# Decoder layer, self attention: the causal mask moved from TensorE products to VectorE's row maximum, on negated scores

## The chip, the cores and the metric

The kernel runs on one core of one Trainium2 chip. The metric is the device time of one execution in microseconds (us), the median of three runs; lower is better.

## What is computed

The reference is one decoder layer over x of shape (4, 1024, 256), float32. Its three parts are a causal self attention, a cross attention over 77 context rows, and a block with latent attention and four experts. Only the first part is changed:

```python
x = x + _L0_attn_ref(_layernorm(x), gamma, w_qkv, w_out)
...
def _L0_attn_ref(x, gamma, w_qkv, w_out):      # 8 heads of 128, 1024 rows
    ...
    q = q * scale_attn                          # 128 ** -0.5
    sim = jnp.einsum('bihd,bjhd->bhij', q, k)
    causal_mask = jnp.triu(jnp.ones((n, n), dtype=bool), k=1)
    sim = jnp.where(causal_mask, neg, sim)
    attn = jax.nn.softmax(sim, axis=-1)
    out = jnp.einsum('bhij,bjhd->bihd', attn, v)
```

## The kernel before

The four batches are worked through one after the other; each passes through self attention, cross attention, latent attention and routing, and after the last batch the expert layers run over all sorted rows. Every engine has an instruction stream of its own, in an order written out by hand, and counts semaphores to wait for the others.

**Self attention.** A batch has 8 heads, numbered 0 to 7. One head has 8 query tiles t = 0 to 7 of 128 rows. Only the causal part of the scores is computed: tile t has n = 128(t+1) columns. For each head TensorE (PE) projects q and k (L910) and v (L920) from the transposed rows. For each tile, `scores` (L926) waits until the exponentials of tile t-2 are done (L933), multiplies q by k into one or two PSUM banks (L937), and adds the causal mask to the last 128 columns by one more product in bf16, of an identity and a 128x128 upper triangle of -3e38 (L940). There are two buffers of two banks each, so tiles t and t+2 share one. A float32 product is two matrix instructions in the trace, and a transpose and the bf16 mask product are one each.

VectorE (DVE) takes the maximum of the n columns, negated, straight from PSUM (`tile_max`, L1424, L1428). ScalarE (ACT) then computes exp(score - maximum) from PSUM into SBUF with its row sum (L744, in `self_exps`). VectorE takes the reciprocal of the sum (L1434) and scales the tile (L1439). In VectorE's order (`head`, L1449) the maximum of tile t stands ahead of the reciprocal and scaling of tile t-1.

**What lies between.** From head 1 on, PE does a piece of the previous head's `products` (L968) after each tile's scores: it transposes 128x128 blocks of the probabilities (`turn_probs`, L955), ScalarE copies them to SBUF (`take_probs`, L735), and PE multiplies them with v (`use_probs`, L965). A head has 12 such pieces u, one in tile 0, one or two in every other. ScalarE's order has the pieces of tile t ahead of the exponential of tile t. After tile 7, PE projects the next head (L910, L920) and ScalarE copies the results out (L719, L723).

**The two ends of a batch.** Head 0 has nothing between its eight tiles (L983). After head 7's tiles PE waits until VectorE has taken head 6's output (L1012, released by L1445, which stands behind head 7's last scaling), then does head 7's products alone.

**Latent attention** masks in VectorE already: `max_chunk` (L1604) uses `tensor_reduce` for full banks (L1618) and, for the last columns, `tensor_tensor_reduce` with `causal_wide` (L1623), a 128x512 float32 constant, which is zero but for the triangle in its last 128 columns. It writes the sum to a scratch tile in SBUF and the maximum to a column.

**The start.** SyncE's queue loads x, then the four tensors of `first_consts` (L222, L483), two heads' weights, and all the other constants, `causal_wide` the first of them. VectorE waits for the other constants at L1400, ahead of head 0.

## Time and profile before

| | |
|---|---|
| median of 3 runs | 2685.35 us (2682.97 to 2687.71) |
| the profiled execution's own time | 2685.82 us |
| its span, first to last instruction | 2684.1 us |
| mean granted TensorE clock | 0.971 |
| PE matmul busy | 2520.5 us (94%) |
| DVE busy | 1383.6 us (52%) |
| ACT busy | 1065.1 us (40%) |
| POOL busy | 313.0 us (12%) |
| chain that ended last, by engine | PE 89%, ACT 3%, issue 3%, DVE 3% |
| mask products, L940 | 256 (4 batches x 8 heads x 8 tiles) |

The profile is of one execution. Matrix instructions overlap each other, so an instruction's duration is longer than the time until the next one starts: what a product costs the engine is read from start to start. "Issue" is time in which an engine waited for nothing that the profile shows. The granted clock is 1 at 2.4 GHz and 0.5 at 1.2 GHz.

### The profile page before, as it was taken

The page shows a single profiled execution, that of the slowest core. Times are in us where ns is not written, and L with a number is a line of the kernel's source. Part 1 is how long each engine was busy: PE and PEld are TensorE (multiplying, and loading weights), DVE is VectorE, ACT ScalarE, POOL GpSimd, SP SyncE. Part 2 cuts the span into 40 slices and gives each one's busy share as a digit, 9 for nine tenths or more (in the row PEclk, how much of TensorE's full clock was granted, in tenths as well). Part 3 has the DMA queues.
Part 4 walks back from the last instruction along what each step waited for, and adds up shares of the span by engine and source line. Part 5 has one row for each costly group of instructions (what it writes and reads, how often), then busy time and mean ns, then how long its engine had stood idle before and what let it go on. Part 6 is the DMA issues. An engine that isn't in the chain of part 4 may idle for free.

```text
span 2684.1 us, 44027 instructions
## 1 busy us (share of the span) xinstructions
PE 2520.5 (94%) x16830; PEld 1680.7 (63%) x16831; DVE 1383.6 (52%) x3834; ACT 1065.1 (40%) x2284; POOL 313.0 (12%) x436
## 2 busy tenths in 40 slices
PE   7999899998999999998999999989999999969998
PEld 4555665664555675664655675655556665649997
DVE  3334377853333477843333477833333578744443
ACT  3444134643444134543444134534443225612221
POOL 2000010212000010211000010220000011231111
PEclk9999999998999999998999999999999999979999
DMA  3000000001000000001000000010000000041111
GB/s 106 13 12 1 16 1 1 2 15 44 12 13 1 16 1 2 2 18 39 15 10 1 16 1 2 2 41 23 12 7 1 16 1 2 2 188 57 53 53 38
DMA packets 33490, 57.30 MB, mean 21 GB/s; under 512 B 7915, under 2 KB 24504, under 8 KB 32920
## 3 DMA queue, kind: packets, MB, share of 16 engines
q1 hardware_dynamic: 28552, 41.73, 5.0%
q0 software_dynamic: 4752, 13.02, 1.3%
q8 instruction: 126, 2.06, 0.3%
q14 instruction: 60, 0.49, 0.1%
HBM read 40.41 MB, written 14.32 MB: 20 GB/s over the span
## 4 chain that ended last, share of the span: by engine, by line
PE 89%; ACT 3%; issue 3%; DVE 3%; another core or an unknown queue 1%; POOL 1%; DMA 0%; DVEq 0%; POOLq 0%
PE ps L1221 11%; PE ps L965 10%; PE ps L937 9%; PE ps L910 8%; PE ps L1251 6%; PE ps L895 6%; PE ps L955 5%; PE ps L1326 5%; PE ps L1340 5%; PE ps L920 4%; PE ps L1186 4%; PE ps L850 3%; PE ps L866 2%; PE ps L1086 1%; PE ps L1070 1%
## 5 line engine op out<-in xcount | busy, mean ns | idle before, releaser
L1428 DVE TENSOR_REDUCE neg_max<-ps 128x1 f32<-128x128 f32 (+7 forms) x256 | 194.1, 758 | 597.6 <-PE ps L940 555.4
L803 ACT ACTIVATE arena<-ps 128x512 f32<-128x512 f32 (+1 forms) x640 | 320.1, 552 | 276.1 <-PE ps L1221 273.3
L1221 PE MATMUL ps<-arena 32*128 32x256 f32 (+1 forms) x2560 | 386.9, 379 | 0.0
L1221 PEld LDWEIGHTS ps<-arena 32*128 32x128 f32 x2560 | 272.9, 184 | 111.8 <-issue 72.3
L1186 PE MATMUL ps<-arena 32*128 32x512 f32 (+3 forms) x1536 | 334.7, 527 | 3.9 <-ACT arena L793 3.9
L937 PE MATMUL ps<-arena 128*128 128x512 f32 (+3 forms) x768 | 304.8, 509 | 25.6 <-ACT arena L744 18.5
L965 PE MATMUL ps<-arena 128*128 128x512 f32 (+3 forms) x768 | 319.2, 503 | 5.5 <-ACT arena L735 1.7
L735 ACT ACTIVATE arena<-ps 128x512 f32<-128x512 f32 (+3 forms) x384 | 188.0, 491 | 296.2 <-PE ps L955 294.2
L937 PEld LDWEIGHTS ps<-arena 128*128 128x128 f32 x768 | 143.9, 197 | 164.3 <-issue 130.6
L910 PE MATMUL ps<-turned_t,arena 128*128 128x512 f32 x512 | 227.7, 598 | 1.1 <-ACT turned_t L706 1.1
L744 ACT ACTIVATE arena<-ps,neg_max 128x128 f32<-128x128 f32 (+7 forms) x256 | 189.0, 738 | 65.6 <-DVE neg_max L1428 46.1
L955 PE MATMUL ps<-ident,arena 128*128 128x128 f32 x1152 | 191.6, 276 | 20.8 <-ACT arena L723 11.4
L955 PEld LDWEIGHTS ps<-ident,arena 128*128 128x128 f32 x1152 | 131.4, 141 | 114.6 <-issue 83.5
L1251 PE MATMUL ps<-arena,mv_rows 128*32 128x256 f32 (+1 forms) x2560 | 188.4, 369 | 2.7 <-POOL arena L646 2.7
L1618 DVE TENSOR_REDUCE arena<-ps 128x1 f32<-128x512 f32 x256 | 164.7, 685 | 42.7 <-PE ps L1186 40.9
L910 PEld LDWEIGHTS ps<-turned_t,arena 128*128 128x128 f32 x512 | 95.7, 192 | 111.2 <-issue 109.7
L646 POOL TENSOR_SCALAR_AFFINE_SELECT arena<-arena 128x1024 f32<-128x1024 f32 x64 | 71.2, 1113 | 606.7 <-ACT arena L803 606.7
L1623 DVE CUSTOM_DVE_ANT_0 arena<-ps,causal_wide 128x128 f32<-128x128 f32 (+3 forms) x256 | 113.1, 488 | 53.6 <-PE ps L1186 53.1
L719 ACT ACTIVATE arena<-ps 128x512 f32<-128x512 f32 x128 | 76.4, 597 | 157.6 <-PE ps L910 154.2
L1623 DVE CUSTOM_DVE_ANT_0 arena<-ps,causal_wide,arena 128x128 f32<-128x128 f32 (+3 forms) x256 | 127.4, 548 | 22.2 <-PE ps L1186 21.6
L580 POOL TENSOR_TENSOR tmp<-mv,c_eps 128x4 f32<-128x4 f32 x34 | 6.8, 201 | 1131.6 <-DVE mv L1376 1131.5
L965 PEld LDWEIGHTS ps<-arena 128*128 128x128 f32 x768 | 116.7, 192 | 34.5 <-issue 17.7
(218 smaller groups left out, 3667.3 us busy)
## 6 DMA issues: line engine op xcount, KB each, us to landing
arena<-in_w_qkv SPq DMA_DIRECT2D x32, 384.0 KB, 3.0
arena<-in_w SPq DMA_DIRECT2D x2, 4096.0 KB, 16.6
xin<-in_x SPq DMA_DIRECT2D x5, 1024.0 KB, 5.6
xres_ids<-sorted_res SPq DMA_DIRECT2D x35, 129.0 KB, 2.3
xin<-sorted_rows SPq DMA_DIRECT2D x35, 128.0 KB
w_out<-in_w_out SPq DMA_DIRECT2D x1, 1024.0 KB
out<-xin,out_row POOLq DMA_INDIRECT x35, 2.9
sorted_res<-xin SPq DMA_DIRECT2D x4, 129.0 KB
```

What stands on the lines that cost most here:

```text
L735: nc.scalar.activation(probs_t[u % 4][:, lo:BANK], ps[:, 4 + u % 2, lo:BANK], ACT.Copy).then_inc(pt_taken, 1)
L744: nc.scalar.activation(probs[par][:, TRI[t]:TRI[t] + n], ps[:, buf:buf + 2, :].rearrange("p a n -> p (a n)")[:, 0:n], ACT.Exp, bias=neg_ma ...
L803: nc.scalar.activation(mprobs_t[n % BUFS][:, j, 0:QUARTER + more], ps[:, item_bank(n, j), 0:QUARTER + more], ACT.Exp).then_inc(mexp_done, 1)
L910: last = nc.tensor.matmul(ps[:, 4 + i % 3, :], w_head[par][:, kt, w:w + HD], turned_t[:, kt, (i % 2) * BANK:(i % 2 + 1) * BANK], start=(kt ...
L937: last = nc.tensor.matmul(ps[:, buf + c // BANK, 0:m], q_t[par][:, t * P:(t + 1) * P], k_t[par][:, c:c + m], start=True, stop=True)
L955: last = nc.tensor.transpose(ps[:, 4 + u % 2, (t - 4 * g) * P:(t - 4 * g + 1) * P], probs[par][:, TRI[t] + kb * P:TRI[t] + (kb + 1) * P], ...
L965: nc.tensor.matmul(ps[:, 6 + g, lo:BANK], v_rows[par][:, kb, :], probs_t[u % 4][:, lo:BANK], start=(kb == 0), stop=True, skip_group_check= ...
L1186: last = nc.tensor.matmul(ps[:, MAX_BANK[m], at:at + n], q_heads_t[rows_j, g, t * P:(t + 1) * P], k_heads_t[rows_j, g, c * BANK:c * BANK + ...
L1221: return nc.tensor.matmul(ps[:, item_bank(n, j), kb * QUARTER:kb * QUARTER + n_q], k_heads_t[rows_j, g, keys_at:keys_at + P], q_heads_t[ro ...
L1251: last = nc.tensor.matmul(ps[SLOT * j:SLOT * (j + 1), 7, QUARTER - n_q:QUARTER], mv_rows[:, 2 * p + kb, GROUP * g + j, :], mprobs_t[n % BU ...
L1428: nc.vector.tensor_reduce(neg_max[:, par, t:t + 1], ps[:, buf:buf + 2, :].rearrange("p a n -> p (a n)")[:, 0:n], AX.X, ALU.max, negate=Tru ...
L1623: last = nc.vector.tensor_tensor_reduce(max_junk[s % 2][:, at:at + n], scores, causal_wide[:, BANK - n:BANK], 1.0, part if c == 1 else MAS ...
```

## The change

The 256 mask products go. ScalarE scales q by -(128 ** -0.5) when it copies it, so PSUM holds negated scores. VectorE adds `causal_wide`, whose triangle now is +3e38, in place in PSUM and takes the row minimum in the same instruction, which is the negated maximum. For tiles 4 to 7, whose columns fill two banks, it first takes the minimum of the full first bank (`tensor_reduce` into `low_part`), waits for that on its own semaphore, and gives it to the second instruction as its starting value. ScalarE's exponential takes scale -1. Latent attention's masked maximum subtracts the constant instead of adding it. Two bf16 constants and their loads ahead of the first weights go.

```diff
@@ constants
-        ident_b = sb("ident_b", [P, P], BF16)
-        causal_b = sb("causal_b", [P, P], BF16)
...
-        first_consts = [(ident, "ident"), (gamma, "gamma"), (ident_b, "ident_b"), (causal_b, "causal_b")]
+        first_consts = [(ident, "ident"), (gamma, "gamma")]
...
+        low_part = sb("low_part", [P, 2])
...
+        low_done = sem("low_done")
@@ take_qkv, ScalarE
                         nc.scalar.activation(dst, ps[:, 4 + i % 3, :], ACT.Copy,
-                                             scale=float(HD) ** -0.5 if i < 2 else 1.0).then_inc(qk_taken, 1)
+                                             scale=-float(HD) ** -0.5 if i < 2 else 1.0).then_inc(qk_taken, 1)
@@ self_exps, ScalarE
-                                             bias=neg_max[:, par, t:t + 1],
+                                             bias=neg_max[:, par, t:t + 1], scale=-1.0,
                                              accum_out=row_sum[:, par, t:t + 1]).then_inc(exp_done, 1)
@@ scores, TensorE
                         m = min(BANK, n - c)
-                        diag = c + m == n
                         last = nc.tensor.matmul(ps[:, buf + c // BANK, 0:m], q_t[par][:, t * P:(t + 1) * P],
                                                 k_t[par][:, c:c + m], start=True, stop=True)
-                        if diag:
-                            last = nc.tensor.matmul(ps[:, buf + c // BANK, m - P:m], ident_b[:], causal_b[:],
-                                                    start=False, stop=True, skip_group_check=True)
                     last.then_inc(scores_done, 1)
@@ tile_max, VectorE
                     dve.wait_ge(scores_done, b * (HEADS * NT) + h * NT + t + 1)
-                    nc.vector.tensor_reduce(neg_max[:, par, t:t + 1],
-                                            ps[:, buf:buf + 2, :].rearrange("p a n -> p (a n)")[:, 0:n],
-                                            AX.X, ALU.max, negate=True).then_inc(max_done, 1)
+                    if t >= HALF:
+                        nc.vector.tensor_reduce(low_part[:, t % 2:t % 2 + 1], ps[:, buf, :], AX.X, ALU.min).then_inc(low_done, 1)
+                        dve.wait_ge(low_done, b * (HEADS * HALF) + h * HALF + t - HALF + 1)
+                        n -= BANK
+                        buf += 1
+                    nc.vector.tensor_tensor_reduce(ps[:, buf, 0:n], ps[:, buf, 0:n], causal_wide[:, BANK - n:BANK], 1.0,
+                                                   low_part[:, t % 2:t % 2 + 1] if t >= HALF else -MASKED, ALU.add, ALU.min,
+                                                   neg_max[:, par, t:t + 1]).then_inc(max_done, 1)
@@ max_chunk, VectorE (latent attention)
-                                                                  part if c == 1 else MASKED, ALU.add, ALU.max,
+                                                                  part if c == 1 else MASKED, ALU.subtract, ALU.max,
@@ arrange, on the host
-        "ident_b": bf16_bits(np.eye(P)),
-        "causal_b": bf16_bits(upper),
-        "causal_wide": np.concatenate([np.zeros((P, BANK - P), np.float32), upper], 1),
+        "causal_wide": np.concatenate([np.zeros((P, BANK - P), np.float32), -upper], 1),
```

## Rows read from the trace of the kernel before

**Rows 1.** The chain of waits from 56 to 267 us (batch 0, heads 1 to 7)
```profile
by line: PE ps L965 27.6%; PE ps L937 25.0%; PE ps L910 19.5%; PE ps L955 13.9%; PE ps L920 10.2%; ACT arena L723 2.0%; PE ps L940 1.3%; issue 0.6%
```
**Rows 2.** The timeline of one head, 150.9 to 173.5 us: start, duration, instruction, idle before
```profile
151.79 0.66 PE L955 MATMUL ps<-ident,arena 128*128 128x128 f32 x4 [0.41 <-ACT arena L723]
152.49 0.60 ACT L735 ACTIVATE arena<-ps 128x512 f32<-128x512 f32 x1 [0.74 <-PE ps L955]
...
153.23 1.10 PE L965 MATMUL ps<-arena 128*128 128x512 f32 x2
...
167.40 0.22 PE L940 MATMUL ps<-causal_b,ident_b 128*128 128x128 bf16 x1
167.46 0.50 PE L955 MATMUL ps<-ident,arena 128*128 128x128 f32 x3
167.66 1.09 DVE L1428 TENSOR_REDUCE neg_max<-ps 128x1 f32<-128x896 f32 x1 [1.94 <-PE ps L940]
...
168.66 0.15 DVE L1434 RECIPROCAL inv_sum<-row_sum 128x1 f32<-128x1 f32 x1
168.78 1.01 ACT L744 ACTIVATE arena<-ps,neg_max 128x896 f32<-128x896 f32 x1 [0.30 <-DVE neg_max L1428]
168.85 0.62 DVE L1439 TENSOR_SCALAR arena<-arena,inv_sum 128x768 f32<-128x768 f32 x1
...
170.85 0.38 ACT L735 ACTIVATE arena<-ps 128x256 f32<-128x256 f32 x1 [0.96 <-PE ps L955]
```
**Rows 3.** Groups of VectorE instructions, shapes kept apart: count, busy us, mean ns, idle before
```profile
L1618 DVE TENSOR_REDUCE arena<-ps 128x1 f32<-128x512 f32 x256 | 164.7, 685 | 42.7 <-PE ps L1186 40.9
L1623 DVE CUSTOM_DVE_ANT_0 arena<-ps,causal_wide,arena 128x512 f32<-128x512 f32 x64 | 45.5, 749 | 14.1 <-PE ps L1186 14.1
...
L1623 DVE CUSTOM_DVE_ANT_0 arena<-ps,causal_wide 128x512 f32<-128x512 f32 x64 | 42.0, 689 | 17.6 <-PE ps L1186 17.3
...
L1428 DVE TENSOR_REDUCE neg_max<-ps 128x1 f32<-128x1024 f32 x32 | 39.2, 1225 | 33.2 <-PE ps L940 33.1
...
L1428 DVE TENSOR_REDUCE neg_max<-ps 128x1 f32<-128x640 f32 x32 | 26.4, 825 | 64.4 <-PE ps L940 63.4 <-remote 1.0
...
L1623 DVE CUSTOM_DVE_ANT_0 arena<-ps,causal_wide,arena 128x128 f32<-128x128 f32 x64 | 22.3, 348 | 2.8 <-PE ps L1186 2.8
L1428 DVE TENSOR_REDUCE neg_max<-ps 128x1 f32<-128x512 f32 x32 | 22.1, 692 | 20.1 <-PE ps L940 15.8 <-remote 4.4
```
**Rows 4.** The timeline of batch 0's head 0, 40 to 44 us
```profile
40.78 0.48 DVE L1439 TENSOR_SCALAR arena<-arena,inv_sum 128x512 f32<-128x512 f32 x1
...
41.27 0.96 DVE L1428 TENSOR_REDUCE neg_max<-ps 128x1 f32<-128x768 f32 x1
...
42.26 0.90 ACT L744 ACTIVATE arena<-ps,neg_max 128x768 f32<-128x768 f32 x1 [0.67 <-DVE neg_max L1428]
...
43.31 1.98 PE L937 MATMUL ps<-arena 128*128 128x512 f32 x4
```
**Rows 5.** The timeline behind the last tile of batch 0's head 7
```profile
269.25 0.68 DVE L1445 COPY arena<-ps 128x512 f32<-128x512 f32 x1
270.04 0.96 PE L955 MATMUL ps<-ident,arena 128*128 128x128 f32 x7 [2.35 <-issue]
```
**Rows 6.** Busy time and granted clock (PEclk) of a stretch, 272 to 276 us
```profile
272.00:276.00 4.00, 4.00 (x16) 2.71 (x15) 0.34 (x2) 0.38 (x1) 0.00 (x0) 0.57 0.00 0
```
**Rows 7.** The longest pieces of the whole chain: the same projection in batches 1 to 3
```profile
881.69 27.89 PE ps L895 x128
1476.10 27.89 PE ps L895 x128
2066.89 27.89 PE ps L895 x128
```
**Rows 8.** The load of x, from the page's DMA issues: count, KB, us to landing
```profile
xin<-in_x SPq DMA_DIRECT2D x5, 1024.0 KB, 5.6
```

## The prediction

> **What bounds the kernel.** I read the table of busy times and the chain's shares first: PE carries the chain for 89% of the span. Then the chain of waits over the stretch of batch 0 that has heads 1 to 7: the lines on it are PE's, save for one ScalarE copy (L723, 2.0%), and VectorE's maximum is not on it. The mask products are, with 1.3% of 211 us, or 2.7 us for 56 of them, about 0.05 us each [rows 1]. So PE paces this stage and the masks are part of the pace. Then I read the timeline of one head, to find what each mask's removal moves and how much room the longer maximum has; last, the two ends of a batch, where the order of work is different.
>
> **The price of a mask product.** Its row says 0.22 us, but the next transposes start 0.06 us behind it (167.40 to 167.46) [rows 2], and the chain's share gives 0.05. I take 0.055 us. The 256 together are 14.1 us, the most that their removal can give. The weight load of the mask lies beside the product ahead of it and is worth nothing. The Trainium skill ("TensorE: Matmul & The Clock Gate", Back-to-back issue gap) puts a load and a 128-column product at about 81 ns in a sustained stream; here the mask's start to start is 0.06 us and the trace decides. By the page's figure the gain summed below would be some 4 us larger.
>
> **Heads 1 to 6, tiles 2 to 7: gained.** PE's instructions stand shoulder to shoulder around these masks: what follows needs only copies that ScalarE made well before. Six masks a head, 0.33 us.
>
> **Tiles 0 and 1: nothing.** Behind tile 0's mask PE sits idle for 0.41 us until ScalarE has copied v (L723), and that copy hangs on the projection ahead of the scores. A shorter score phase makes this wait longer. Tile 1's mask lies between the transposes of piece 0, whose copy runs from 152.49 to 153.09, and its product at 153.23, which starts 0.14 us after the copy's end; the transposes between, three at 0.11 from 152.78, end at 153.11 [rows 2]. So that product too is timed by ScalarE.
>
> **The new maximum.** Tiles 0 to 3: one masked reduction in place of one reduction. At 512 columns the rows have 0.689 against 0.692 us [rows 3], so no cost. The accumulator's read-out follows each, with its start under the end of the main instruction; I count 0.01 us for it. Tiles 4 to 7: a reduction over 512 columns (0.685), a wait on VectorE's own semaphore, and the form with a starting value from memory. The price of the wait I take from the pair of L1434 and L1439, where the second needs the first: 168.66 + 0.15 = 168.81, second at 168.85, so 0.04 us. Tile 7: 0.685 + 0.04 + 0.749 + 0.01 = 1.484 against 1.225 us, +0.26. Tile 4: 0.685 + 0.04 + 0.348 + 0.01 = 1.083 against 0.825, also +0.26 [rows 2, 3]. The maximum also starts 0.055 us earlier, as no mask product comes between, so ScalarE gets it 0.20 us later against PE's work in tiles 4 to 7.
>
> The Trainium skill ("VectorE: DVE Perf Modes", The DRAIN you can't avoid) says that a semaphore between chained operations costs nothing extra. The trace disagrees: the reciprocal without a wait starts at 168.66 while the maximum (167.66 + 1.09) ends at 168.75, an overlap of 0.09, and the pair with a wait has a gap of 0.04 [rows 2]. By the rule a tile would cost 0.13 us less.
>
> What no row shows is a VectorE write into PSUM. Lower bound: nothing less than the SBUF scratch form (a gain of up to 0.06 a tile, the difference between the forms 0.749 and 0.689, is not excluded). Upper bound: the main instruction takes a second pass, doubling it. The nearest rows are the same instruction with the same PSUM source [rows 3]; I take no surcharge and keep both ends.
>
> **Is it covered in heads 1 to 7?** The exponential of tile 6 waits 0.30 us for the maximum already, ends at about 169.9 with its read-out, and ScalarE is next wanted at 170.85 for a copy that PE needs [rows 2]. Room: about 0.9 us, used: 0.20. The cover is ScalarE's idle time there; were it gone, PE would wait for the copy one for one. In tile 7 the next copy is behind four instructions of the next projection, with a room of about 1 us; in tiles 4 and 5 more, since the exponential of tile 5 stands behind two copies anyway. VectorE is idle 1.94 us ahead of tile 6's maximum. Price: nothing.
>
> **Head 0: a loss.** Here nothing stands between the tiles, and PE waits for exponentials. Three masks lie on the chain ahead of tile 4's maximum (tiles 0, 2, 4), so it starts 0.16 earlier. It lasts 0.26 longer and ends 0.10 later. On VectorE tile 3's scaling follows, and tile 5's maximum stands right behind that: 40.78 + 0.48 = 41.26, start 41.27 [rows 4]. So it starts 0.10 late and ends 0.36 late. Tile 5's exponential, which waits for it (0.67 us), is 0.36 late, and tile 7's scores, which need it and until now started just as PE came free, go from 43.31 to 43.67. Less tile 7's mask, PE leaves head 0 0.30 us later. Times 4 batches: +1.2 us.
>
> **Head 7: a wash.** Five masks (tiles 2 to 6) bring its last scores forward by 0.28 us. Then PE waits for VectorE's L1445 (269.25 + 0.68, PE at 270.04, idle 2.35 us) [rows 5], which follows tile 7's maximum, exponential and scaling. That chain loses 0.055 and gains 0.26. Sum -0.07, times 4: -0.3 us. PE's idle time there grows from 2.35 to about 2.6 us.
>
> **The rest.** Negative scale on ScalarE, subtract for add in latent attention: same instructions, nothing (an effect of either sign would need 0.01 us on each of 512 masked maxima, and these mostly hide under PE). Two loads of 32 KB fewer behind x: x takes 5.6 us for 1024 KB and is issued first [rows 8]; if the loads shared its bandwidth, 64/1024 of 5.6, or 0.35 us. I take nothing. Loads behind them are issued earlier and were not waited for.
>
> **Sum.** Heads 1 to 6: 24 x 0.33 = -7.9. Head 0: +1.2. Head 7: -0.3. Together -7.0 us. Against the profiled execution's 2685.82 us (its span and 1.7 around it) that is 2678.8; that execution was 0.5 above the median, so against the median 2678.3. I say **2678.5**.
>
> **The clock.** After head 7's idle time the clock fell to its lower level, 0.57 on average over 4 us, so 3.4 us at 1.2 GHz, which costs PE 1.7 us [rows 6]. The stretches are not the same in all batches: from projection to projection batch 1 to 2 took 594.4 us and batch 2 to 3 590.8 [rows 7]. Any shift of the work can add or take such a stretch. I count 2 us either way.
>
> **Rivals.**
> 1. *Gain not regained.* PE is paced around the masks by ScalarE's copies, as in tiles 0 and 1, and removal only lengthens waits. For it: it is so in two tiles of eight. Against it: the masks' share of the chain [rows 1]. With half of the 7.9 lost: -3.1, 2682.2. Chance 0.2.
> 2. *The in-place write costs a second pass (slower).* Place: the chain maximum, exponential, scores of head 0, and the end of head 7. At 1.04 ns a column ((0.749 - 0.348)/384) a pass costs 0.29 us in tile 0, 0.56 in tile 2, 0.69 in tile 3, 0.48 in tile 5, 0.61 in tile 6, 0.75 in tile 7. Heads 1 to 6 would still hide it, just (0.20 + 0.61 of the 0.9 us in tile 6). In head 0 tiles 0 and 2 are on the chain, tile 3 stands behind tile 2 on VectorE, and tile 5's scores hang on tile 3: 0.29 + 0.56 + 0.69 + 0.48 = 2.0 us; head 7 adds tile 7's 0.7. Sum: -7.0 + 8.0 + 2.8 = +3.8, 2689.2. It decides from 0.65 of a second pass on (7.0 of 10.8); past a whole one tile 6 shows in 24 heads too. For it: no row shows the write. Against: nothing in the masked form, which also writes 512 columns, costs more than the plain reduction [rows 3]. Chance 0.07.
> 3. *A milder surcharge*, 0.1 to 0.2 us an instruction: by the same four tiles head 0 adds 0.4 to 0.8, head 7 0.1 to 0.2: +2 to +4, so 2680.3 to 2682.3. Chance 0.13.
> 4. *More is gained*: tile 1's mask counts too, and the accumulator pair runs better than its rows. 24 x 0.055 = 1.3 more, and with the 0.13 us of the wait given back in head 0 and 7 about 1 more: -9.3, 2676. Chance 0.1.
> That the masks stay on PE is not possible: their line is gone.
>
> **The numbers.** My forecast, 2676 to 2681, has 0.5. The range 2673.5 to 2685.5 takes in it, rivals 1, 3 and 4 and the clock. About 0.2% (5.4 us) is what a measurement of this kernel can tell from no change; so faster means below 2680.0. Of the forecast 0.42, of rival 4 all 0.1, of rivals 1 and 3 0.04: faster 0.56. Slower (over 2690.7): the part of rival 2 past a whole pass and little else, 0.04. Same: 0.40.
>
> **What would show it.** No L940 in the list; a steady head (scores of tile 0 to the same in the next) shorter by 0.33 us; tile 0's idle time before L955 up from 0.41 to 0.47; masked minimum of 512 columns near 0.69 and 0.75 us; tile 4 to 7's exponentials 0.2 later against PE's work; head 0's projections starting 0.3 later; idle time before L955 at the batch's end 2.6 us. Wrong, if a head is not 0.33 us shorter, or if the in-place form of 512 columns takes over 0.85 us.

## The result, and the profile after

Six executions of each kernel on one chip: 2669.95 us after (2669.04 to 2675.04) against 2684.92 before (2681.45 to 2687.71), ratio 0.9948 with a 95% interval of 0.9935 to 0.9961. That is 15.0 us less (10.5 to 17.5), where 7 were forecast. It is faster by more than the 0.2% bound, and below the range. The profiled execution took 2669.12 us.

The page of the kernel after, its span, the busy times and the shares of the chain:

```profile
span 2667.4 us, 43897 instructions
...
PE 2501.4 (94%) x16574; PEld 1671.2 (63%) x16575; DVE 1417.6 (53%) x4218; ACT 1067.1 (40%) x2284; POOL 312.3 (12%) x436
...
PE 89%; ACT 3%; DVE 3%; issue 3%; POOL 1%; DMA 0%; another core or an unknown queue 0%; SPq 0%; DVEq 0%; POOLq 0%
```

TensorE keeps its 89% of the chain. Lines have moved: scores L936, transposes L951, the products with v L961, the two halves of the maximum L1425 and L1429, VectorE's scaling L1440 and its copy L1446.

The maximum's groups after, shapes kept apart (count, busy us, mean ns, idle before), with latent attention's L1624 for comparison; they answer to [rows 3]:

```profile
L1425 DVE TENSOR_REDUCE low_part<-ps 128x1 f32<-128x512 f32 x128 | 88.5, 691 | 170.9 <-PE ps L936 164.3 <-remote 6.7
L1624 DVE CUSTOM_DVE_ANT_0 arena<-ps,causal_wide,arena 128x512 f32<-128x512 f32 x64 | 45.5, 748 | 14.1 <-PE ps L1182 14.1
L1624 DVE DVE_READ_ACCUMULATOR2_ANT arena<- 128x1 f32 x512 | 42.4, 83 | 0.0
L1624 DVE CUSTOM_DVE_ANT_0 arena<-ps,causal_wide 128x512 f32<-128x512 f32 x64 | 42.0, 688 | 16.2 <-PE ps L1182 15.9
L1429 DVE DVE_READ_ACCUMULATOR2_ANT neg_max<- 128x1 f32 x256 | 36.3, 142 | 0.0
...
L1429 DVE CUSTOM_DVE_ANT_0 ps<-ps,causal_wide,low_part 128x512 f32<-128x512 f32 x32 | 24.3, 759 | 1.1
L1429 DVE CUSTOM_DVE_ANT_0 ps<-ps,causal_wide 128x512 f32<-128x512 f32 x32 | 22.4, 699 | 15.5 <-PE ps L936 13.0 <-issue 2.5
```

The write back into PSUM costs 0.011 us at 512 columns (699 against 688, 759 against 748). The read-out of the accumulator takes 0.142 us against 0.083. There is no second pass over the columns.

The timeline of one head after, which answers to [rows 2] (start, duration, instruction, idle before):

```profile
151.22 0.66 PE L951 MATMUL ps<-ident,arena 128*128 128x128 f32 x4 [0.46 <-ACT arena L723]
...
164.02 0.56 DVE L1440 TENSOR_SCALAR arena<-arena,inv_sum 128x640 f32<-128x640 f32 x1
...
164.49 0.69 DVE L1446 COPY arena<-ps 128x512 f32<-128x512 f32 x1
...
166.58 0.49 PE L951 MATMUL ps<-ident,arena 128*128 128x128 f32 x3
166.78 0.69 DVE L1425 TENSOR_REDUCE low_part<-ps 128x1 f32<-128x512 f32 x1 [1.61 <-PE ps L936]
...
167.51 0.63 DVE L1429 CUSTOM_DVE_ANT_0 ps<-ps,causal_wide,low_part 128x384 f32<-128x384 f32 x1
...
168.05 0.14 DVE L1429 DVE_READ_ACCUMULATOR2_ANT neg_max<- 128x1 f32 x1
...
168.23 1.01 ACT L744 ACTIVATE arena<-ps,neg_max 128x896 f32<-128x896 f32 x1 [0.63 <-DVE neg_max L1429]
...
169.91 0.38 ACT L735 ACTIVATE arena<-ps 128x256 f32<-128x256 f32 x1 [0.58 <-PE ps L951]
...
173.24 0.60 ACT L719 ACTIVATE arena<-ps 128x512 f32<-128x512 f32 x1 [0.77 <-PE ps L910]
...
204.62 0.60 ACT L719 ACTIVATE arena<-ps 128x512 f32<-128x512 f32 x1 [0.77 <-PE ps L910]
```

Tile 0's wait for v grew from 0.41 to 0.46 us. Tile 6's exponential now waits 0.63 us for the maximum, against 0.30, and the copy behind it still had 0.58 us of ScalarE's idle time ahead of it. So the longer maximum is hidden. It is longer than forecast: the exponential starts 1.65 us behind PE's next transposes (166.58 to 168.23), where it was 1.32 (167.46 to 168.78 in [rows 2]), so 0.33 us later against PE's work and not 0.20. A head, from L719 to L719, takes 31.38 us; before it took 31.75 (174.18 to 205.93).

Head 7's end, which answers to [rows 5]:

```profile
267.53 0.68 DVE L1446 COPY arena<-ps 128x512 f32<-128x512 f32 x1
...
268.32 1.33 PE L951 MATMUL ps<-ident,arena 128*128 128x128 f32 x7 [2.68 <-issue]
```

Idle 2.68 us where 2.6 was forecast. In batch 0 the stage is nearly as forecast, and four times that is about 7.5 us. The rest does not show there. The projection that opens cross attention answers to [rows 7]:

```profile
285.19 27.89 PE ps L895 x128
874.82 27.89 PE ps L895 x128
1465.89 27.89 PE ps L895 x128
2056.23 27.89 PE ps L895 x128
```

Before, the last three began at 881.69, 1476.10 and 2066.89. The lead is 6.9, 10.2 and 10.7 us there and 16.7 at the end (2684.1 less 2667.4). So 6.0 us of it come behind the last self attention, where the change does nothing. Another 3.3 us lie in batches 1 and 2: from head 0's first copy to head 7's the kernel after is 1.8, 3.6, 3.4 and 1.9 us shorter in batches 0 to 3. The surplus of batches 1 and 2 is in head 0, which starts late there in both kernels, by an amount that differs from execution to execution (below). The stretch behind the last self attention, latent attention of batch 3 up to the experts, first in the kernel before and then in the kernel after (us, busy time of PE, PEld, DVE, ACT, POOL, granted clock, DMA share, GB/s):

```profile
2180.84:2413.72 232.88, 204.46 (x1960) 127.59 (x1958) 155.73 (x514) 103.53 (x210) 45.59 (x58) 0.91 0.14 53
```
```profile
2170.00:2397.18 227.18, 198.27 (x1960) 124.45 (x1958) 155.71 (x514) 103.50 (x210) 45.72 (x59) 0.94 0.15 55
```

The same 1960 products take 5.7 us less, at a granted clock of 0.94 against 0.91, so with fewer of its microseconds at the level of 1.2 GHz. The stage's own gain (7.8, below), head 0's delays (3.3) and this stretch (5.7) make up the 16.7 us between the two profiles; the differences elsewhere cancel.

### The profile page after: what moved, and what is told of

Read it like the earlier page. It is cut to its first block, busy times and chain, and to the rows that moved or that the text cites. A ratio compares the mean times of both kernels' runs of the same rounds, so it can differ in the third digit from the quotient of the medians.

```text
span 2667.4 us, 43897 instructions
## 1 busy us (share of the span) xinstructions
PE 2501.4 (94%) x16574; PEld 1671.2 (63%) x16575; DVE 1417.6 (53%) x4218; ACT 1067.1 (40%) x2284; POOL 312.3 (12%) x436
## 4 chain that ended last, share of the span: by engine, by line
PE 89%; ACT 3%; DVE 3%; issue 3%; POOL 1%; DMA 0%; another core or an unknown queue 0%; SPq 0%; DVEq 0%; POOLq 0%
PE ps L1217 11%; PE ps L961 10%; PE ps L936 9%; PE ps L910 8%; PE ps L1247 6%; PE ps L895 6%; PE ps L951 5%; PE ps L1322 5%; PE ps L1336 5%; PE ps L920 4%; PE ps L1182 4%; PE ps L850 3%; PE ps L866 2%; PE ps L1082 1%; PE ps L1066 1%
## 5 line engine op out<-in xcount | busy, mean ns | idle before, releaser
L936 PE MATMUL ps<-arena 128*128 128x512 f32 (+3 forms) x768 | 305.6, 511 | 24.6 <-ACT arena L744 17.5
L961 PE MATMUL ps<-arena 128*128 128x512 f32 (+3 forms) x768 | 320.5, 504 | 5.8 <-ACT arena L735 1.4
L1429 DVE CUSTOM_DVE_ANT_0 ps<-ps,causal_wide 128x128 f32<-128x128 f32 (+3 forms) x128 | 63.9, 500 | 375.5 <-PE ps L936 335.5
L936 PEld LDWEIGHTS ps<-arena 128*128 128x128 f32 x768 | 144.9, 198 | 168.2 <-issue 134.4
L951 PEld LDWEIGHTS ps<-ident,arena 128*128 128x128 f32 x1152 | 144.6, 142 | 126.8 <-issue 89.2
L951 PE MATMUL ps<-ident,arena 128*128 128x128 f32 x1152 | 191.0, 276 | 23.7 <-ACT arena L723 13.0
L1425 DVE TENSOR_REDUCE low_part<-ps 128x1 f32<-128x512 f32 x128 | 88.5, 691 | 170.9 <-PE ps L936 164.3
L961 PEld LDWEIGHTS ps<-arena 128*128 128x128 f32 x768 | 117.0, 192 | 41.0 <-issue 24.2
L1624 DVE CUSTOM_DVE_ANT_0 arena<-ps,causal_wide 128x128 f32<-128x128 f32 (+3 forms) x256 | 113.1, 488 | 52.3 <-PE ps L1182 51.8
L1624 DVE CUSTOM_DVE_ANT_0 arena<-ps,causal_wide,arena 128x128 f32<-128x128 f32 (+3 forms) x256 | 127.3, 547 | 22.2 <-PE ps L1182 21.6
L1440 DVE TENSOR_SCALAR arena<-arena,inv_sum 128x128 f32<-128x128 f32 (+7 forms) x256 | 133.4, 521 | 10.5
```

The costliest lines, as they stand in the source:

```text
L936: last = nc.tensor.matmul(ps[:, buf + c // BANK, 0:m], q_t[par][:, t * P:(t + 1) * P], k_t[par][:, c:c + m], start=True, stop=True)
L951: last = nc.tensor.transpose(ps[:, 4 + u % 2, (t - 4 * g) * P:(t - 4 * g + 1) * P], probs[par][:, TRI[t] + kb * P:TRI[t] + (kb + 1) * P], ...
L961: nc.tensor.matmul(ps[:, 6 + g, lo:BANK], v_rows[par][:, kb, :], probs_t[u % 4][:, lo:BANK], start=(kb == 0), stop=True, skip_group_check= ...
L1624: last = nc.vector.tensor_tensor_reduce(max_junk[s % 2][:, at:at + n], scores, causal_wide[:, BANK - n:BANK], 1.0, part if c == 1 else MAS ...
```

## The experiments

Theory A: the change's own effect is what its rows say (about -7.5 us), and the rest is the granted clock in stretches that it does not touch. Rival B: the mask products cost TensorE more than 0.06 us each, or lower its clock, and the 15 us are the change's own. Later a third matter came in: late releases at the start of batches 1 to 3.

The runs, in five sessions, each on one chip (1 and 3 on the same one; clock: median of the granted clock of the single executions; of before only the session's median):

| session, before | kernel | median us | clock | ratio to before, 95% interval |
|---|---|---|---|---|
| 1: 2660.05 | mask products out (e1) | 2642.16 | 0.978 | 0.9939 [0.9926, 0.9952] |
| | products kept, with zeros (e2) | 2653.81 | 0.9795 | 0.9983 [0.9972, 0.9994] |
| | first bank early (e3) | 2640.13 | 0.980 | 0.9926 [0.9912, 0.9939] |
| | after again (e4) | 2640.90 | 0.981 | 0.9941 [0.9924, 0.9959] |
| 2: 2684.4 | before again (e5) | 2684.95 | 0.972 | 1.0002 [0.9993, 1.0011] |
| | before, later start (e6) | 2686.57 | 0.973 | 1.0011 [1.0003, 1.002] |
| | after, later start (e7) | 2673.93 | 0.974 | 0.9971 [0.9954, 0.9989] |
| | after, filled (e8) | 2682.07 | 0.974 | 0.9987 [0.9978, 0.9996] |
| 3: 2685.66 | before, scatters later (e9) | 2685.45 | 0.975 | 0.9994 [0.9984, 1.0004] |
| | after, scatters later (e10) | 2676.42 | 0.9755 | 0.997 [0.9958, 0.9982] |
| | early bank, scatters later (e11) | 2674.62 | 0.9745 | 0.9962 [0.9947, 0.9977] |
| | after, scatters spread (e12) | 2641.68 | 0.980 | 0.9834 [0.9822, 0.9847] |
| 4: 2688.93 | before, scatters spread (e13) | 2661.22 | 0.976 | 0.9893 [0.9876, 0.9909] |
| | after, scatters spread (e14) | 2641.08 | 0.981 | 0.9828 [0.981, 0.9846] |
| | early bank, spread (e15) | 2641.01 | 0.979 | 0.9815 [0.9799, 0.9832] |
| | before once more (e16) | 2687.65 | 0.971 | 0.9997 [0.9988, 1.0007] |
| 5: 2659.75 | after, spread, filled (e17) | 2657.87 | 0.9765 | 0.9991 [0.9975, 1.0007] |
| | before, spread, filled (e18) | 2653.40 | 0.9805 | 0.9986 [0.9971, 1.0001] |

The kernel before is itself at two levels, 2660 in sessions 1 and 5 and 2684 to 2689 in the others. The ratio compares the executions of one session; it is not the quotient of the two medians, and differs from it by up to 0.0013. It carries whatever clock the session's executions had.

### One part alone: the products

e1, on the kernel before:

```diff
-                        if diag:
-                            last = nc.tensor.matmul(ps[:, buf + c // BANK, m - P:m], ident_b[:], causal_b[:],
-                                                    start=False, stop=True, skip_group_check=True)
```

It leaves the mask of self attention out. In e2 the products are there, but their triangle holds zeros.

> The kernel before with the 256 mask products left out and nothing else changed; self attention is then not causal inside the diagonal block of each tile, and that part of the computation is left out. Theory A (each product is worth its 0.055 us on PE's path, in tiles 0 and 1 too): a steady head is 0.43 to 0.44 us shorter, 7 heads and a shorter chain in head 0 give 3.3 us a batch, 13 us in all, about 2672, give or take 3 us for where the clock's lower level falls. Theory B (as predicted: tiles 0 and 1 give nothing): a steady head is 0.33 shorter, 10 us in all, 2675. Theory C (the gain came from the VectorE form or the two loads, not from the products): under 5 us, 2680 or more.

e2, on the changed kernel, with the two loads put back:

```diff
+                        if diag:
+                            last = nc.tensor.matmul(ps[:, buf + c // BANK, m - P:m], ident_b[:], causal_b[:],
+                                                    start=False, stop=True, skip_group_check=True)
...
+        "causal_b": bf16_bits(np.zeros((P, P), np.float32)),
```

> The changed kernel with the 256 products and the two loads put back, the triangle of the product filled with zeros, so that PE's work is that of before and VectorE's that of after. Theories A and B: no gain is left; the longer maximum costs 0.7 us in head 0 and 0.3 at the end of head 7, 1.0 us a batch, 4 us in all: about 2689. Theory C: it keeps most of the gain, 2675 or less.

In e1 a head takes 31.38 us and head 7's end 32.64 instead of 33.02; in e2 a head takes 31.76. So the products are worth 0.37 us a head, 0.061 for each of the six that count, in either kernel. The totals are off what was expected: e1 is 17.9 us under before by the medians, where 10 to 13 were expected, and e2 6.2 under, where 4 over was. e2's products are there to see:

```profile
L942 PE MATMUL ps<-causal_b,ident_b 128*128 128x128 bf16 x256 | 56.1, 219 | 0.0
```

And e2 ran at a clock of 0.9795, above that of the kernel before (0.976). So the products are not what holds the kernel before at 0.976. In both pairs that differ in the products, the kernel without them has the higher median clock (0.978 against 0.976, 0.981 against 0.9795), by 0.0015 to 0.002; that they have no part in the clock is not shown.

### An earlier first bank, and the kernel after again

```diff
+                        if t >= HALF and c == 0:
+                            last.then_inc(low_scored, 1)
...
-                    dve.wait_ge(scores_done, b * (HEADS * NT) + h * NT + t + 1)
                     if t >= HALF:
+                        dve.wait_ge(low_scored, b * (HEADS * HALF) + h * HALF + t - HALF + 1)
```

> The changed kernel, but VectorE takes the minimum of the first bank as soon as that bank's product is done, while PE works on the second. If the longer maximum costs time at the end of head 7 and in head 0, as theory A and B hold, about 0.7 us come back at each head 7 and 0.2 to 0.4 in each head 0: 3.8 us in all, 2666, and PE's idle time at the batch's end falls from about 2.7 to 2.0 us. If the maximum is hidden everywhere: no change, 2670.

> The changed kernel once more, unchanged, as the measure for the others on this chip and for how its stages vary from execution to execution. 2670, within 2 us. If the clock's lower level falls where it did in the first profile, the batches take the same times to 0.3 us; if it falls elsewhere, single stages differ by steps of about 1.7 us.

e3 shortened the two places that it was made for, by less than expected: head 7's end from 33.0 to 32.5 us (0.7 expected), head 0's tiles from 10.8 to 10.6. Its median is 0.8 us under e4's. e4 gave 19 us under before by the medians (16 by the ratio) on a chip where both kernels were 25 to 30 us lower than in the first comparison. Of its twelve executions ten took 2638.7 to 2642.2 us at clocks of 0.980 and 0.981, and two 2658.1 and 2661.3 at 0.974 and 0.973. One kernel, 20 us apart, by the clock.

### Position in time, and filling the wait

e5 is the kernel before. e6 and e7 begin with four small loads more (the first work is 1.9 us later); e8 adds three warm-up products to each batch of the changed kernel:

```diff
+            for i in range(4):
+                sp.dma_start(rows[:, i, 0:KT], d["gamma"]).then_inc(first_in, 16)
             load_rows(0)
...
                 pe.wait_ge(xkv_taken, b * 3 + 3)
+                keep_warm(3, 3)
                 project(PROJ_SELF, ...
```

> The kernel before once more, for a second profile of it, and for more executions with their mean granted clock. Executions of one kernel with the same mean clock should agree within 1 us. Theory D (beyond 10 us, the gain is the clock: more of the kernel before runs at the lower level): its mean clock is 0.004 to 0.005 below that of the changed kernel on the same chip in most executions, and its profile shows extra stretches at the lower level, at the start of a batch or in the last routing, as the first profile did. Rival (the change saves 15 us of work): the mean clocks agree, and the steady heads or other stages account for all.

> The kernel before with four small loads ahead of the load of x, so that all work starts about 1.9 us later. If the position of the work in time decides where the clock falls, its mean clock changes from that of the kernel before by 0.002 or more and the time moves by something other than 1.9 us. If it doesn't: the same clock, and 1.9 us more.

> The changed kernel with the same four loads in front. Same clock as the changed kernel and 1.9 us more if position doesn't matter; a mean clock lower by 0.003 to 0.005 and up to 10 us more if it does.

> The changed kernel with three warm 512-column products on PE before the output projection of self attention in each batch, 2.6 us a batch, so that a batch is as long as before the change. Without an effect of the clock it takes back all of the work saved: 10.3 us more than the changed kernel at the same mean clock. If the change's extra gain comes from how long a batch is, its mean clock falls to that of the kernel before, and it takes 15 to 20 us more than the changed kernel. If it comes from what the self attention does, the clock stays.

e5 gave 1.0002; its executions at 0.972 take 2683.8 to 2686.9, so those of one clock do not agree within the 1 us that was expected. e6 took 2686.57, about the 1.9 us of its loads over before (0.8 to 5.4 by the interval), at the same clock. e7 came out at 0.9971, 7.8 us under before (2.9 to 12.3), with those loads in it; against e6, which has them too, it is 12.6 us lower by the medians and 10.7 by the ratios. So the 15 us were a little less here, with an interval that reaches the first one. e8 did not change the clock, and its median is 8.1 us over e7's: with e7's 1.9 us of loads that is the 10 us of work put back.

What the profiles of session 2 showed instead was head 0. In batch 0 its tiles take 10.5 us (10.9 with the change), in batches 1 to 3 between 20.5 and 23.2, with and without it. The two profiles of the first comparison have it too (21.0 to 23.2 us). The timeline of the kernel before in batch 1:

```profile
618.89 0.96 POOL L669 DMA_INDIRECT sorted_rows<-rows,arena  x1 [0.30 <-issue]
619.78 0.60 ACT L723 ACTIVATE arena<-ps 128x512 f32<-128x512 f32 x1 [3.62 <-remote]
...
621.21 0.29 DVE L1428 TENSOR_REDUCE neg_max<-ps 128x1 f32<-128x128 f32 x1 [11.92 <-remote]
...
622.05 1.65 PE L937 MATMUL ps<-arena 128*128 128x384 f32 x2 [3.92 <-ACT arena L744]
...
630.48 0.69 DVE L1428 TENSOR_REDUCE neg_max<-ps 128x1 f32<-128x512 f32 x1 [3.25 <-PE ps L940]
...
632.00 0.20 POOL L674 TENSOR_TENSOR lists_pause<-c_half 128x8 f32<-128x8 f32 x1 [2.01 <-DMA sorted_res<-xres_ids,arena]
```

Scores that were finished wait 1 to 4 us for the engine that takes them, all engines in turn, for as long as GpSimd issues the 16 indirect scatters of the batch before (L669 and L671, one every 1.27 us). Behind them the rows are normal.

### Moving the scatters

```diff
                 pool.wait_ge(route_ready, b + 1)
+                if b < BATCH - 1:
+                    pool.wait_ge(exp_done, (b + 1) * (HEADS * NT) + NT)
```

> The kernel before; POOL issues the 16 indirect scatters of the first three batches not at once but after the last exponential of head 0 of the next batch, so during head 1's projection and tiles. Head 0's tile stage (first score to the last turn of head 0) took 22.3 us in batch 1 of the profiled execution of before and 10.5 in batch 0, where nothing is scattered. Theory A, the late releases follow the scatters: head 0 takes 10.5 us in all four batches and head 1 of batches 1 to 3, 31.8 us from L719 to L719 in batch 0, takes the 11 us more; the total stays within 5 us of before (2679 to 2690 where before is at 2684.5). Theory B, it is the clock or the start of a batch: head 0 keeps its 22 us, head 1 its 31.8, the total that of before. Theory C, scatters hurt only beside head 0's projection: head 0 10.5 and head 1 31.8, the total 30 to 35 us under before (near 2651). On a chip where head 0 takes 10.5 us in every batch of before, all three give the time of before within 2 us, except for runs of before that had one such stage (11 us each).

> The changed kernel with the same move of the scatters. Against the kernel with the move alone it isolates the change with head 0 undisturbed in all four batches: theory of the rows, head 0 +0.44, six heads -0.37, head 7 -0.05, times four batches, is -7.5 us (-6 to -9.5). If the change's larger gain (15 us on the first chip) came from head 0's disturbed stages, it shrinks to this here; the rival, that the change itself saves 13 to 15 us in the self attention, expects -13 to -15 against the moved kernel before. Against before itself: theory A -7.5 or a little less, theory C -38 to -43 us.

ScalarE's copies of q and k in e9, batch 1 (one of the four of each head is shown):

```profile
616.53 0.60 ACT L721 ACTIVATE arena<-ps 128x512 f32<-128x512 f32 x1 [7.39 <-PE ps L912]
...
638.06 0.59 ACT L721 ACTIVATE arena<-ps 128x512 f32<-128x512 f32 x1
...
680.62 0.60 ACT L721 ACTIVATE arena<-ps 128x512 f32<-128x512 f32 x1 [1.09 <-PE ps L912]
```

Head 0 to 1 takes 21.53 us where it took 33.43 (608.62 to 642.05), and head 1 to 2 takes 42.56 where it took 31.16. The delay went with the scatters, in all three batches of e9 and e10. The total did not move (0.9994), as theory A there had it. e10 is 9.0 us under e9 by the medians (by the two ratios 2 to 11), where 6 to 9.5 were expected and rival B had 13 to 15.

> The changed kernel with the minimum of the first bank started as soon as that bank is scored, and with the scatters moved. The early minimum took head 0 from 10.94 to 10.60 us and the end of head 7 from 33.0 to 32.5 in one profile each: (0.34 + 0.4) x 4 is -3.0 us, and it measured about 2 to 2.7 us under the changed kernel. Expected 2 to 3 us under the changed kernel with the move; were the early minimum worth nothing, the same as it.

e11 is 1.8 us under e10 (2 to 3 expected), inside the noise of the two.

e12 lets a pair of scatters go after each of heads 0 to 3, three after each of heads 4 and 5, and two after head 6:

```diff
                 for t in range(NT):
+                    if b < BATCH - 1:
+                        pool.wait_ge(exp_done, (b + 1) * (HEADS * NT) + NT * (t // 2 + 1))
                     nc.gpsimd.indirect_dma_start(d["sorted_rows"], ...
                 for t in range(NT):
+                    if b < BATCH - 1 and t % 3 == 0:
+                        pool.wait_ge(exp_done, (b + 1) * (HEADS * NT) + NT * (t // 3 + 5))
                     nc.gpsimd.indirect_dma_start(d["sorted_res"], ...
```

> The changed kernel; the 16 scatters of each of the first three batches are spread over the next batch's heads: one row scatter pair after each of heads 0 to 3, three of the others after each of heads 4 to 6 (the last two with head 6). Theory A with a cost for each scatter in progress (11 us over 16): the same 11 us for a batch in small parts, the total that of the changed kernel. Theory A where the cost lies in a burst that starves the releases: one or two scatters hide, head 0 takes 10.9 us, and each batch gains up to 11 us, 30 us in all on a chip where before's head 0 takes 22 us. Theory B: no difference.

2641.68 us, 44 under before (41 to 48), by far the largest gain up to here. The delay is gone from all batches. Three copies of its batch 1 again (22.23 and 30.42 us apart):

```profile
611.28 0.60 ACT L723 ACTIVATE arena<-ps 128x512 f32<-128x512 f32 x1 [9.66 <-PE ps L914]
...
633.51 0.59 ACT L723 ACTIVATE arena<-ps 128x512 f32<-128x512 f32 x1
...
663.93 0.60 ACT L723 ACTIVATE arena<-ps 128x512 f32<-128x512 f32 x1 [0.77 <-PE ps L914]
```

So it is the burst that delays releases, and not each scatter. Chance is a poor rival: in sessions 3 and 4 all four profiles with the burst have the delay in all three batches (e9 to e11, e16), and all four without it (e12 to e15) in none. And 2641.68 is what the kernel after took in session 1 without this edit. In all profiles of that session head 0's tiles took 10.1 to 11.2 us in every batch: there the burst delayed nothing, on the same chip as in session 3. The level of 2660 us that the kernel before has in sessions 1 and 5 is that of e13 below, which has no late releases; no profile of before itself was taken there, so that its head 0 is undisturbed in sessions 1 and 5 is inferred.

### Both kernels without the late releases

> The kernel before with the scatters of the first three batches spread over the next batch's heads, as e12 has them on the changed kernel (2641.7 us). Head 0 should take 10.5 us and heads 1 to 6 31.75 in every batch. If the change's own effect is what its rows say (-7.5 us), this runs at e12's kernel + 7.5, near 2649; if the 15 us of the first comparison are the change's own, near 2656.

> The kernel of e12 again, beside e13 on one chip: 2641.7 as before, whatever the chip and whatever the kernel before measures there (2660 or 2685), if the disturbance is gone from it. A rival, that e12 fell in an undisturbed stretch by chance, expects head 0 or one of the next heads at 10 us more in some batches and 2655 to 2675 here.

Batch 1 in both profiles, ScalarE's first copy of head 0 and that of head 7, e13 and then e14:

```profile
611.03 0.60 ACT L723 ACTIVATE arena<-ps 128x512 f32<-128x512 f32 x1 [9.71 <-PE ps L914]
...
822.50 0.60 ACT L723 ACTIVATE arena<-ps 128x512 f32<-128x512 f32 x1 [1.09 <-PE ps L914]
```
```profile
607.97 0.60 ACT L723 ACTIVATE arena<-ps 128x512 f32<-128x512 f32 x1 [9.04 <-PE ps L914]
...
817.55 0.60 ACT L723 ACTIVATE arena<-ps 128x512 f32<-128x512 f32 x1 [0.77 <-PE ps L914]
```

211.47 against 209.58 us: -1.89 for heads 0 to 6, and head 7's end gives 0.05 more. Four batches are -7.8 us. PE itself, from its first score to the next projection, spends 10.82 us in head 0 instead of 10.44. But the medians differ by 20.1, and neither 2649 nor 2656 came out for e13. Its six executions are 2652.9 and 2655.3 (clock 0.979 and 0.978) and four of 2661.1 to 2663.4 (0.975 and 0.976); of e14's five, four are 2639.8 to 2641.2 (0.980 and 0.981) and one 2650.1 (0.977).

The whole chains show where a batch differs, by the start of cross attention's first projection, e13 and then e14:

```profile
287.17 27.89 PE ps L899 x128
871.74 27.89 PE ps L899 x128
1452.55 27.89 PE ps L899 x128
2036.28 27.89 PE ps L899 x128
```
```profile
284.80 27.89 PE ps L899 x128
867.17 27.89 PE ps L899 x128
1447.20 27.89 PE ps L899 x128
2025.63 27.89 PE ps L899 x128
```

Batches of one kernel in one execution, with the same work and no late releases, take 584.6, 580.8 and 583.7 us in e13 and 582.4, 580.0 and 578.4 in e14. The work of the change is 1.9 of it. One place where this happens is the one that the prediction priced, from PE's restart behind head 7 to the output projection. In e14 it takes 17.32 us in batch 1 and 15.63 in batch 3, with the same work:

```profile
849.85:867.17 17.32, 15.96 (x72) 10.08 (x73) 2.74 (x7) 5.78 (x12) 0.00 (x0) 0.90 0.00 0
...
2010.00:2025.63 15.63, 14.28 (x72) 9.21 (x72) 2.74 (x7) 5.77 (x12) 0.00 (x0) 1.00 0.00 1
```

The lower level costs its 1.7 us there, or does not come at all. Of the 28 such stretches in before, after and e12 to e16, 22 take 16.8 us or more and six 15.63. A stretch of latent attention in batch 3 of e13, then the same one in e14:

```profile
2171.00:2185.00 14.00, 14.00 (x32) 3.87 (x31) 6.66 (x18) 0.00 (x0) 0.00 (x0) 0.63 0.00 0
```
```profile
2161.00:2175.00 14.00, 14.00 (x45) 4.34 (x46) 9.26 (x22) 0.00 (x0) 0.00 (x0) 0.88 0.00 1
```

In both TensorE shows as busy throughout (14.00 of 14.00); one had the clock at 0.63 of full speed and got through 32 products, the other at 0.88 and through 45. In the 6 us ahead of it PE was busy for 4.78 and 5.06 us, at a clock of 1.00.

> The changed kernel with the first bank's minimum started early and the scatters spread. The rows of e11 give -0.4 us for head 0 and -0.43 for the end of head 7, times four is -3.3 us: expected 2 to 3.3 us under e14, near 2639.

> The kernel before, for its profile in this call: if its median is near 2660, head 0 takes 10.5 us in most batches; if near 2685, about 22 us in batches 1 to 3. The rival, that the two levels come from the clock elsewhere (latent attention or routing), expects head 0 the same at either level.

e15 has e14's median (2 to 3.3 us less was expected) and the lowest ratio of all, 0.9815 (45 to 54 us under before), inside e14's interval. Its rows have the early minimum's gain (head 7's end 32.54 against 32.97), its executions the lower clock (0.979 against 0.981). e16 shows batch starts of 32.4 to 35.0 us from L719 to L719 in batches 1 to 3: at 2687 us head 0 is delayed, as in the other sessions at this level.

### The same work added to both

```diff
                 pe.wait_ge(xkv_taken, b * 3 + 3)
+                keep_warm(2, 3)
                 project(PROJ_SELF, ...
```

> The changed kernel, scatters spread, with two more warm-up products (0.86 us each) ahead of the output projection of each batch: 1.7 us x 4 = 6.9 us of work. If time is work, 2641 + 6.9 = 2648 at the same granted clock of 0.981. If the stretches at the lower clock elsewhere decide, the clock moves as well (0.976 to 0.981) and the median falls anywhere between 2648 and 2661.

> The kernel before, scatters spread, with the same two products. If time is work, 2661 + 6.9 = 2668 at a clock of 0.976, 20 us over e17. If the low stretches elsewhere decide, the two kernels at the same granted clock differ by 7.5 us, and this one's clock may rise above 0.976 with more work in it, the median then falling between 2655 and 2668.

"Time is work" wanted 2648 and 2668, 20 us apart. Measured: 2657.87 and 2653.40. **With these two products in both kernels, no gain of the change is left in the times**: its median is 4.5 us above the other, and the intervals of the two ratios (0.9975 to 1.0007, 0.9971 to 1.0001) lie on each other, so neither is shown to be faster. The one without it has a median 8 us under e13, which has less work; their executions overlap (2649.7 to 2665.1, 2652.9 to 2663.4). The clocks have changed sides: 0.9765 with the change, 0.9805 without. e17's executions are one of 2640.4 (clock 0.983), two near 2648.2 (0.979) and nine of 2656.4 to 2659.5 (0.976 and 0.977).

In e17's profile the stretch behind head 7 keeps the full clock in batches 1 and 2:

```profile
849.20:866.65 17.45, 16.09 (x77) 10.08 (x78) 3.91 (x12) 5.78 (x12) 0.00 (x0) 1.00 0.01 1
```

With 1.8 us of work more than e14's 15.63 it takes 0.13 us more than e14's 17.32. So added work can take a stretch at the lower level away from one place.

At one and the same clock the order is the expected one. I put a straight line through all single executions of the kernels without late releases (sessions 1 and 5, and e12 to e15), with one slope for all and an offset for each kernel; e13 counts as the kernel before, since by itself it lies 0.3 ± 0.5 us from it. A thousandth of granted clock is worth 2.5 us, and the spread about the line is 1.2 us (with late releases, in sessions 2 and 3, such lines have 1.7 to 2.0 us a thousandth). The offsets against the kernel before, with one standard error, beside four times what the rows of batch 1 give (a filled stretch is 1.82 us longer at full clock, 17.45 against 15.63):

| kernel | offset, us | rows times four |
|---|---|---|
| after (e4, e12, e14) | -8.0 ± 0.4 | -7.8 |
| mask products out (e1) | -12.7 ± 0.5 | -11.8 |
| products kept (e2) | +3.2 ± 0.4 | +3.9 |
| early bank (e3, e15) | -10.0 ± 0.5 | -10.3 |
| before, filled (e18) | +5.2 ± 0.4 | +7.3 |
| after, filled (e17) | -1.8 ± 0.4 | -0.5 |

The filled kernels are 1.3 and 2.1 us off their rows, which stays open. For the change itself the line agrees with the rows, and the sessions with late releases give the same: a line through e6 and e7 has 8.7 ± 0.7 us between them, one through e9 and e10 8.6 ± 0.9.

Three executions of the kernel before at 0.981 say it directly: 2649.2 to 2649.4 us, where e4 and e14 at 0.981 take 2638.7 to 2642.2. The other 12 of the 20 us between the medians are the clock: where there are no late releases the kernel after has a median of 0.980 or 0.981 in three sessions (e4, e12, e14), and the kernel before 0.976 in three (1, 5 and e13). So that part came back each time, but two more products a batch undo it.

## Why the prediction was wrong

- **The self attention: right.** -7.0 was forecast, the rows of e13 and e14 give -7.8 and the line -8.0 ± 0.4. A product is worth 0.061 us rather than 0.055, so a head gained 0.37 instead of 0.33 us. That tiles 0 and 1 give nothing held: tile 0's wait is 0.46 us (0.47 forecast).
- **Head 0: right in kind, a little small.** PE leaves it 0.38 us later where nothing disturbs it, and 0.45 in batch 0 (10.49 to 10.94), with 0.30 forecast. Over both heads 0 and 1, from copies to copies, e13 has 52.70 us (611.03 to 663.73) and e12 52.65.
- **Head 7: right**, -0.05 a batch (-0.07 forecast), idle 2.68 us (2.6).
- **The new maximum: hidden as forecast, its length too small.** The instructions take 0.699 and 0.759 us where 0.689 and 0.749 were taken. But the read-out of 0.142 us ends 0.05 us behind the main instruction (168.05 + 0.14 against 167.51 + 0.63), not 0.01. And the maximum does not start 0.055 us earlier against PE's work: it starts 0.20 us behind the next transposes in both kernels (167.46 to 167.66, 166.58 to 166.78). Together the exponential is 0.33 us later instead of 0.20, which the room of 0.9 us still covers. Rival 2 is out, and so is rival 3. The wait before the second half was priced well: it starts at 167.51 behind 166.78 + 0.69 = 167.47, a gap of 0.04. A copy that waits for no result of VectorE's starts 0.09 us before the end of the instruction ahead of it (164.49 against 164.02 + 0.56). The Trainium skill ("VectorE: DVE Perf Modes", The DRAIN you can't avoid) has eight chained copies take the same time with a semaphore after each as with one after the last; between these unlike instructions the rows show a difference of 0.13 us.
- **Rival 1** (gain not regained) fell with the steady head. **Rival 4** (-9.3) fell as well: the work did -7.8, nearer to the forecast, and tile 1's mask is worth nothing (from tile 0's transposes to piece 0's product 1.44 us in both kernels).
- **"I count 2 us either way": this step failed**, the term for the clock. I saw one stretch at the lower clock in one place, 1.7 us, and the spread of two batches of 3.6 us [rows 7], and took it for noise about the sum. The price of that place was right; that there are many such places, each there or not, was left out. By the executions above the clock is worth from 0 to 20 us in the same kernel, and the two kernels need not draw alike, even in the median. Between the two profiles of the first comparison it gave 5.7 us to the change, in one stretch. With 20 us within reach by the clock alone, a range of 12 us was too narrow. That the work came out within 1 us of its forecast does not make the forecast of the total a good one.
- **Batches 1 to 3 were not read.** All rows of the forecast came from batch 0. A look at batch 1 would have shown head 0 at 22 us instead of 10.5. This is the second step that failed: the sum takes head 0 as +0.30 us in all four batches, and in the first comparison's profiles the changed kernel left it 1.3 and 1.2 us earlier in batches 1 and 2 (21.04 against 22.34, 22.05 against 23.21) and 0.3 later in batch 3. Over more profiles the delay varies as much within one kernel, so this too is chance and no gain of the change. And the stretch was worth four times the change.

Open is what decides which executions catch the lower level, and why two products a batch shift it. It was not the mask products alone (e2), nor the start of the program (e6). Open too is why the burst of scatters delays releases in sessions 2, 3 and 4 and not in 1: sessions 1 and 3 ran on the same chip.

## What to carry to other kernels

Work out a small change from the rows of its own stage, and then check the measured difference at equal granted clock, over single executions: medians can differ by over twice the change (20 us against 8), or show none of it, with its own stage the same each time. Read the same stage in every pass of the loop, not in the first one alone; the largest loss here sat at the start of batches 1 to 3. If GpSimd issues indirect DMAs in a burst beside a stage in which engines hand over to one another every microsecond, spread them.

## What was not expected of the hardware

- While GpSimd issues 16 indirect scatters, one every 1.27 us, other engines get their releases 1 to 4 us late (L723 3.62, PE 3.92 us), in some sessions; head 0's tiles go from 10.5 to about 22 us. Two or three scatters at a time do no such harm (e12).
- The granted clock can stand at the lower level while TensorE shows as busy: 0.63 over 14 us of latent attention with PE busy 14.00 of 14.00, after 6 us with PE busy for 4.78 and the clock at 1.00. The ends of products are modelled in these rows; about half of the time there goes to latent attention's scores, products of 32 rows, the rest mostly to warm-up products.
- The same stretch behind head 7 runs at a clock of 0.90 in one batch and 1.00 in another of the same execution, 17.32 and 15.63 us.
- A masked minimum written in place into PSUM costs 0.011 us more than into SBUF, and its accumulator's read-out 0.142 against 0.083 us.
